# Adding matmuls with unread results in front of TensorE's waits in a two-part cross-attention kernel

## What is computed

```python
# first part: grouped attention, 32 query heads, 8 key heads of 16
q = x @ Wq + bq; k = ctx @ Wk + bk; v = ctx @ Wv + bv
x = layernorm(softmax(q k^T / 4 + mask) v @ Wo + bo + x) * gamma + beta
# second part: two layers of 16 heads of 128, one extra key (bias_k, bias_v) each
for i in (1, 2):
    h = layernorm(x) * scale_i + offset_i
    x = x + cross_attention(h, ctx, wq_i, wk_i, wv_i, wo_i, ...)
h = layernorm(x) * scale + offset
out = x + gelu(h @ w_fc1 + b_fc1) @ w_fc2 + b_fc2
```

## Time and profile before

| | |
|---|---|
| median of 3 runs | 2483.79 us (2483.16 to 2483.86) |
| profiled execution | 2484.73 us |
| span of its trace | 2482.8 us |
| mean granted TensorE clock | 0.987 |
| PE busy | 2372.5 us (96%) |
| DVE, ACT, POOL busy | 1232.4, 867.0, 815.4 us |

### The profile page before, as it was taken

The page is one execution under the profiler, slowest core; times in us unless marked ns, Lnnn a source line. Parts: engine busy times, 40 slices in busy tenths (PEclk is TensorE's granted clock), DMA queues, the critical chain, the costliest instruction groups (busy, mean ns, idle before and its releaser), DMA issues.

```text
span 2482.8 us, 38737 instructions
## 1 busy us (share of the span) xinstructions
PE 2372.5 (96%) x14768; PEld 2038.6 (82%) x14768; DVE 1232.4 (50%) x2041; ACT 867.0 (35%) x2499; POOL 815.4 (33%) x598
## 2 busy tenths in 40 slices
PE   6888999999999999989989889999999999998999
PEld 5677888888888888878867778888888888887787
DVE  6985333344533334465679853333354333434654
ACT  5964222222422222232269542222233222223321
POOL 5974223233422323230049542223243222323100
PEclk8998999999999999999999999999999999999999
DMA  4102111012110101201220021111111110110110
GB/s 177 36 10 81 35 34 59 34 42 73 35 35 34 42 34 42 72 34 60 98 102 10 10 81 34 42 51 44 49 56 35 34 42 34 42 51 13 60 43 34
DMA packets 37764, 120.06 MB, mean 48 GB/s; under 512 B 3616, under 2 KB 3872, under 8 KB 37664
## 3 DMA queue, kind: packets, MB, share of 16 engines
q1 hardware_dynamic: 37664, 118.69, 13.8%
HBM read 114.48 MB, written 4.19 MB: 48 GB/s over the span
## 4 chain that ended last, share of the span: by engine, by line
PE 82%; POOL 7%; DVE 5%; ACT 3%; issue 2%; DMA 0%; SPq 0%; POOLq 0%; DVEq 0%; ACTq 0%
PE PS L563 69%; PE PS L794 4%; PE PS L810 4%; PE PS L802 2%; POOL XN L422 1%; POOL W L446 1%; POOL P0D L422 1%; POOL X L456 1%; POOL HF L422 1%; POOL XN L415 1%; ACT AT L1126 1%; POOL W L385 1%; ACT PS L1126 1%; PE PS L785 1%; DVE HB L1654 1%
## 5 line engine op out<-in xcount | busy, mean ns | idle before, releaser
L563 PE MATMUL PS<-AT,W 128*128 128x512 f32 x2496 | 611.9, 396 | 11.2 <-DVE AT L1421 9.5
L563 PEld LDWEIGHTS PS<-AT,W 128*128 128x128 f32 x2496 | 473.4, 191 | 117.5 <-DVE AT L1421 13.4
L485 POOL TENSOR_TENSOR PR<-PR,RC 128x512 f32<-128x512 f32 x128 | 133.3, 1042 | 977.8 <-DVE RC L1506 977.8
L1300 DVE TENSOR_TENSOR X<-PS,X 128x512 f32<-128x512 f32 x416 | 286.2, 690 | 298.0 <-PE PS L563 290.6
L563 PE MATMUL PS<-CT,W 128*128 128x512 f32 x1632 | 410.6, 401 | 14.9 <-DVE CT L1295 10.5
L563 PE MATMUL PS<-W,CX 128*128 128x512 f32 x1632 | 398.1, 397 | 7.9 <-DVE Q L1325 4.2
L563 PE MATMUL PS<-W,CT 128*128 128x256 f32 x3072 | 384.9, 284 | 0.0
L563 PEld LDWEIGHTS PS<-W,CT 128*128 128x128 f32 x3072 | 372.6, 191 | 1.3 <-issue 0.8
L563 PEld LDWEIGHTS PS<-W,CX 128*128 128x128 f32 x1632 | 300.6, 188 | 74.9 <-issue 8.1
L563 PEld LDWEIGHTS PS<-CT,W 128*128 128x128 f32 x1632 | 300.0, 190 | 74.5 <-issue 11.1
L1153 ACT ACTIVATE CX<-PS,VEC 128x512 fp32r<-128x512 f32 x128 | 88.1, 689 | 670.1 <-PE PS L810 670.1
(11 more groups left out here) (108 smaller groups left out, 2460.6 us busy)
## 6 DMA issues: line engine op xcount, KB each, us to landing
RAW<-in_wq SPq DMA_DIRECT2D x44, 512.0 KB, 4.4
RAW<-in_wo SPq DMA_DIRECT2D x44, 512.0 KB, 3.2
RAW<-in_wk SPq DMA_DIRECT2D x40, 512.0 KB, 3.3
RAW<-in_wv SPq DMA_DIRECT2D x40, 512.0 KB, 3.5
raw_c<-in_cT SPq DMA_DIRECT2D x8, 512.0 KB, 5.8
raw_x<-in_xT SPq DMA_DIRECT2D x8, 512.0 KB, 5.8
BVR<-in_bv_rows SPq DMA_DIRECT2D x8, 512.0 KB, 3.7
X<-in_x SPq DMA_DIRECT2D x4, 1024.0 KB, 11.4
```

What stands on the lines that cost most here:

```text
L485: nc.gpsimd.tensor_tensor(PR[:, :, 0:P], PR[:, :, 0:P], RC[:, 0, 0:BT].unsqueeze(2).to_broadcast([P, BT, P]), ALU.mult).then_inc(norm_done, 1)
L563: ins = nc.tensor.matmul(out, lhs(c, a), rhs(c, b), start=(k == 0), stop=(k == total - 1))
L1300: V_.tensor_tensor(X[:, tile, :], PS[:, bank, :], X[:, tile, :], ALU.add).then_inc(done, 1)
```

## The change

Three calls of two new helpers are added to TensorE's stream, and one wait. `fill` writes matmuls of 128x512 with operands from `CT`'s high part (fp32r) into a bank, each one starting the bank anew; `fill_first` does the same with the cleared `VP` in fp32, as the context isn't there yet, and waits for `zeros_done`. Nothing reads what they write. Six are put in front of the first `k0`, in the first half only; sixteen in front of `norm_t` of the second block at the border to the second part, in both halves; fourteen behind `norm_t` in the MLP's first blocks, in both halves, with a wait for the first four GELU results so that bank `BA` is free.

```diff
+            def fill(bank, count):
+
+                for k in range(count):
+                    nc.tensor.matmul(PS[:, bank, :], CT[:, 0, k % C, 0:P], CT[:, 0, k % C, 0:BTOK], start=True, stop=True)
+
+            def fill_first(bank, count):
+
+                pe.wait_ge(zeros_done, 1)
+                zeros = VP[:, 0:2].rearrange("p a h d -> p (a h d)")
+                for _ in range(count):
+                    nc.tensor.matmul(PS[:, bank, :], zeros[:, 0:P], zeros, start=True, stop=True)
...
                 if hf:
                     down(hf - 1, FG // 2 - 1, 2)
+                else:
+                    fill_first(BPT, 6)
                 k0(0)
                 q0(0)
                 values0(0)
...
                         weigh(b0, 0, 0)
                         pe.wait_ge(v_ev, b0 * 2 + 4)
                         pe.wait_ge(k_ev, b0 * 2 + 3)
+                        fill(BA, 16)
                         norm_t(norm_index(hf, ly), 1, BANKS_TURN)
                         transposes(b0, 1)
                         queries(b0 + 1, 1, 0, lq, at_now + 4)
...
                 hidden(0, 1, True)
                 down(hf, 0, 0, True, range(2))
                 norm_t(norm_index(hf, LAYERS), 1, BANKS_MLP)
+                pe.wait_ge(gelu_done, hf * FG * TB * 2 + 4)
+                fill(BA, 14)
                 down(hf, 0, 0, True, range(2, BT))
                 down(hf, 0, 1, True)
                 hidden(0, 2, True)
```

## The result

| | before | after |
|---|---|---|
| median (13 runs each, taken together) | 2483.79 us | 2477.99 us |
| lowest and highest | 2482.16, 2485.97 | 2475.59, 2481.65 |
| ratio, 95% interval | | 0.9975, 0.9967 to 0.9984 |
| profiled execution, span | 2484.73, 2482.8 | 2477.38, 2475.6 |
| mean granted clock | 0.987 | 0.992 |

The change makes the kernel 5.8 us faster (0.2%; the interval lies clear of 1); 7.1 were forecast. The profiled pair lies 7.35 us apart.

A forecast was written before the change was run, and what follows sets the result against it. PE, holding 82% of the chain of waits, was taken to bound the kernel; terms 0 + 2.9 + 2.0 + 2.2 + 0 = 7.1 us off 2483.79 gave 2476.7 us, with a range of 2471 to 2483 us.

The forecast's parts named there:

- The first half's term: First border: fast transposes and an earlier end after the sixteen fills gain 2.9 us, bounds 2.8 to 3.6, 1.4 with late fills.
- about 0.22 us for one: Price of a border or MLP fill at full clock, from chains of 12 projections; 16 cost 3.5 us.
- The second half's 2.0: Second half's border: transposes go from 3.47 to 1.91 us and the border gains 2.0 us, bounds 1.1 to 2.4.
- The 2.2 us of the first half: First half's MLP: with the clock held, 36 matmuls take 8.61 instead of 10.78 us; bounds 0 and 2.2.
- second half: nothing to gain: Second half's MLP: 36 matmuls already take 8.61 us behind a 3.07 us pause; term 0, up to +0.1 us.
- The term 0: Start: six fills shorten the first projection but gain nothing overall; bounds -0.5 and +0.7 us, +1.9 with fills low throughout.
- PE would only idle for 1.7 us more ahead of it, so its 4.61 us, mostly low, stay.: Start: the second projection, released by POOL's split of the query weights, keeps its start at 16.84 and its length.
- transposes count for nothing: Rival, chance 0.03: transposes run low whatever the clock and don't help hold it; 4.5 us gained, 2479.3 us.
- Fills at the low clock: Rival, chance 0.09: added matmuls don't raise or hold the clock; +3.4 us, 2487.2 us, or 2489.4 with another low stretch.
- Lowered elsewhere: Rival, chance 0.23: later pauses meet the clock otherwise and two more low stretches hit full work; -3.4 us, 2480.4 us.
- all held: Rival, chance 0.10: both borders' second pause passes at full clock, the rest loses two low stretches; 11.9 us less, 2471.9.
- the sign of being wrong that was named: Second half's attention stages: new low stretches there in the profile after would count against the forecast.

The follow-up runs named there:

- e1: The kernel after with only the six fills before the first projection left of the change: 2484.90 us, ratio to before 1.0006.
- e3: The kernel after with only the fourteen fills in the MLP left, in both halves: 2481.03 us, ratio to before 0.9989.
- e0: The kernel after itself, unchanged, run again on one chip with other kernels: 2478.20 us, ratio to before 0.9970.
- e2: The kernel after with only the sixteen fills at the border left, in both halves: 2477.62 us, ratio to before 0.9979.
- e7: The kernel after with other forms of fill at the border and in the MLP, sizes and numbers kept: 2477.39 us, one execution.
- e9: The kernel after without the six fills in front of the first projection: 2476.39 us, ratio to before 0.9964.
- e8: The kernel after with more fills: thirteen and twelve in the first half, ten before the MLP in both halves: 2473.67 us, ratio to before 0.9953.
- e5: The kernel after with eight instead of sixteen fills at the border: 2477.80 us, one execution.
- e6: The kernel after with twenty-four instead of sixteen fills at the border: 2481.63 us, one execution.
- e4: The kernel after with 32 fp32 transposes replacing the sixteen border fills, and no fills at the two other places: 2475.78 us, one execution.

## Why the prediction was right, point by point

Direction and size came out inside the range, 5.8 us against 7.1, and at the border and in the first half's MLP by the mechanism that was argued. That the total is so near is partly luck: a gain in the second half's MLP and a loss at the start, both put at nothing, offset one another. Three stretches, measured over the profiled executions, show the terms more surely than one pair does.

PE's timeline before at the two borders, weighing and next unit's scores:

```profile
207.60 1.11 PE L810 MATMUL PS<-PT,V 128*128 128x128 f32 x8
...
226.02 1.06 PE L794 MATMUL PS<-K,Q 128*128 128x129 f32 x8
...
1438.21 1.11 PE L810 MATMUL PS<-PT,V 128*128 128x128 f32 x8
...
1455.67 1.16 PE L794 MATMUL PS<-K,Q 128*128 128x129 f32 x8
```

- **Border, from the weighing to the next unit's scores.** Without fills 18.42, 17.46 (before), 18.45, 18.42 (e1), 18.28, 18.60 (e3), mean 18.3 us. With sixteen, in after, e0, e2, e7 and e9, between 15.80 and 16.24 us, and 16.69 and 16.11 in e8; mean 16.1. A gain of 2.2 us per border, 4.4 in both; the forecast was 2.9 + 2.0 = 4.9. The first half's term was 0.3 us too large in the profiled pair (18.42 - 15.80 = 2.6). The fills end 0.45 us late and not 0.1: the step "about 0.22 us for one" mis-sized a fill that takes 0.236 (in the profile before, too, 12 projections lie between 21.29 and 24.10, 0.234 each). This was offset in part by the second pause, passed at the full clock where a fall was expected. The second half's 2.0 was 1.3 in the pair because before was at its luckiest there.
- **MLP, 36 matmuls.** With fourteen 8.56 to 8.64 us in each of the 16 stretches of after, e0, e3, e5, e6, e7, e8 and e9. Without, first half: 10.78 (before), 10.77, 10.17, 10.17; second half 8.61 (before), 11.28, 10.03, 8.62, in before, e1, e2, e4. The 2.2 us of the first half are 1.9 on the mean, and the step "second half: nothing to gain" was wrong: its pause of 3.07 us loses the clock in two of four executions (0.50 over 2316 to 2322 us in e1, 0.59 and 0.56 over 2308 to 2312 in e2, 1.00 throughout in before and e4), 1.0 us on the mean. I took one execution's 1.00 for a property of the pause.
- **The six.** The term 0 was the step that failed in its sign: "PE would only idle for 1.7 us more ahead of it, so its 4.61 us, mostly low, stay." They don't stay by themselves; in four of five starts without the six the second projection takes 3.0 us. In the profile after the clock falls at 16.9 us (0.73 over 16 to 18 us), 0.2 us behind the end of the longer pause that the shorter first projection leaves, and in e0, e1, e5 and e7 between 0.1 us before that end and 1.0 us behind it; whether the pause's length or the moment of the earlier rise decides stays open (above). It costs 1.6 us in the executions in which it decides; the medians put it at +1.3 (e1_first) and +1.8 (e0_after less e9_no_first), neither clear of zero by itself.

4.4 + 1.9 + 1.0 - 1.3 to 1.8 = 5.5 to 6.0 us, and 5.8 were measured. The means rest on four to twelve stretches each, so that they meet to a few tenths is more than they can promise. The forecast's 7.1 had the border and the first half's MLP nearly right, and lacked the gain in the second half's MLP and the cost of the six.

**Of the rivals**, "transposes count for nothing" fell with e4_transposes (32 of them in 3.71 us, with the clock at 1.00). "Fills at the low clock" fell: the fp32 fills took 7.42 us and were over at 10.03, so that they ran at the low rate for a part only (six would take an estimated 10.6 us low throughout, by the prediction's 1.77 us for one), and none at the border or in the MLP ran low (16 in 3.93 us, 14 in 3.43, at 1.00). "Lowered elsewhere" and "all held" aren't exclusive: low stretches do move. After has new ones at 78, 146 and 1420 us, lacks those of before at 195, 1062, 1308 and 1376 (the lowest window of 2 us in each reads 0.50 to 0.56, the same windows of the other profile 1.00), and the one at 1277 to 1280, now at 1270 to 1276, is 3.4 us longer. Those at 195 and 1420 lie on the same work, the first block's queries just ahead of a border: before has it in the first half only, after in the second. No new one came in the attention stages of the second half, the sign of being wrong that was named, though the one at 1270 got longer. Up to the second border of the profiled pair these moves gave 0.9 us more (the weighing there comes 5.9 us sooner, and 2.8 + 2.2 us had been gained by the unit behind the first border and in the MLP). The "all held" course comes at single borders: with sixteen, the second pause was passed at the full clock in the first half of after, e2, e7 and e9 and in the second half of e2, 15.80 to 15.82 us each, and with a fall in the other seven, 16.09 to 16.69 us. e4's second border had it too, 15.55 us, the shortest of all. What sets where the low stretches of the attention stages fall was not tried; the spread of the runs after (6 us between lowest and highest, with mean clocks of 0.990 to 0.993) fits it, but that is argued and not shown.

## What to carry to other kernels

Filling a pause of TensorE with matmuls nobody reads paid here where the work behind it was on the chain and the fill ended about when the pause did: 1 to 2.2 us a place on the mean, and at the border 24 instead of 16 gave all of it back, while 8 were as good as 16. Count from start to start (0.236 us a fill here, where 16 have a length of 3.93 us) to size the fill, and stay short of the pause. Shortening work in front of a pause can cost more than it gives: behind the longer pause at this kernel's start the second projection was mostly slow (4.55 to 4.61 us in five of six executions, 3.02 in the other), though the totals put the cost at 1.3 and 1.8 us, neither clear of zero. And one execution's clock in a pause says little about the others: behind 3.06 to 3.07 us of pause the second half's MLP took 8.61, 11.28, 10.03 and 8.62 us.

## What was not expected of the hardware

Eight matmuls (1.9 us of work in a pause of 4.6 us) kept the clock at 1.00 up to and through the tile's transposes as well as sixteen, in both halves of the one execution. fp32 matmuls on a cleared operand, all zeros, brought PE to the full rate like others, by their lengths (the granted clock reads 1.00 from the start): the six took 7.42 us in the profile after and 8.49 in e6_24, against an estimated 10.6 us at the low rate throughout (six times the prediction's 1.77), and the first projections behind them 3.00 us instead of 4.62. And in front of the second projection, a pause of 0.9 to 1.5 us left the clock up in all four executions that had it (the projection took 2.99 to 3.03 us), while of seven with 1.75 to 3.4 us, six lost it (4.55 to 4.61 us). In the second half's MLP a pause of 3.07 us kept it in two of four (8.61 and 8.62 us against 10.03 and 11.28).
